# In the first attention of a perceiver kernel, the steps whose low halves VectorE makes move by one place

## The reference

```python
x = x + _L0_xattn_ref(_layernorm(x, axis=-1), ctx_1024, mask_SxS2_ik0, L0_xattn_W_q, L0_xattn_W_k, L0_xattn_W_v, L0_xattn_W_o)
...
x = x + _L1_xattn_ref(_layernorm(x, axis=-1), ctx_1024, L1_xattn_Wq, L1_xattn_Wk, L1_xattn_Wv, L1_xattn_Wo, L1_xattn_bo)
```

## Time and profile before

| | |
|---|---|
| time, median of 3 runs | 423.71 us (423.68 to 423.8) |
| profiled execution, its own time | 421.03 us |
| its span | 419.0 us |
| PE busy | 385.3 us, 92% |
| DVE busy | 317.9 us, 76% |
| ACT busy | 287.4 us, 69% |
| POOL busy | 203.5 us, 49% |
| low halves on POOL (L589) | 67 of 1892 ns |
| low halves on DVE (L589) | 25, median 1083 ns, mean 1214 ns |

### The profile page before, as it was taken

One profiled execution on the slowest core, in us unless ns is written; L12 is line 12 of the kernel. 1 busy time (PEld: TensorE's weight loads), 2 busy tenths in 40 slices (PEclk: granted clock), 3 DMA queues, 4 the chain that ended last, 5 costly groups with the idle time before them and its releaser, 6 DMA issues.

```text
span 419.0 us, 11758 instructions
## 1 busy us (share of the span) xinstructions
PE 385.3 (92%) x4649; PEld 300.2 (72%) x4649; DVE 317.9 (76%) x868; ACT 287.4 (69%) x569; POOL 203.5 (49%) x128
## 2 busy tenths in 40 slices
PE   6788999999999999998988999999999998999975
PEld 3356777777767778887965677767777777888774
DVE  3788888888886887735769999999988887544544
ACT  3377888888787886645428798888899886533240
POOL 2467879879865551001001558889666660030000
PEclk9799999999999999999999999999999999999989
DMA  8889798999999998970004999999999999600000
GB/s 314 311 235 179 134 175 133 178 142 184 237 172 233 226 164 159 408 285 0 5 0 88 170 155 197 200 195 181 200 193 191 190 193 196 265 2 3 4 0 5
DMA packets 186567, 68.11 MB, mean 163 GB/s; under 512 B 181376, under 2 KB 182160, under 8 KB 185616
## 3 DMA queue, kind: packets, MB, share of 16 engines
q1 hardware_dynamic: 186224, 66.31, 78.5%
q10 hardware_dynamic: 288, 1.05, 0.7%
HBM read 21.90 MB, written 0.03 MB: 52 GB/s over the span
## 4 chain that ended last, share of the span: by engine, by line
PE 43%; DVE 29%; issue 9%; ACT 8%; DMA 7%; POOL 2%; SPq 1%; DVEq 0%; POOLq 0%; ACTq 0%
PE ps L519 14%; DVE probs L613 14%; PE ps L487 12%; DMA probsT<-halves 5%; ACT probs L556 3%; PE ps L748 3%; DVE probsT L642 3%; DMA moe<-in_ctxT 2%; DVE U L631 2%; PE ps L499 2%; PE ps L1080 2%; DVE den L626 2%; ACT halves L563 1%; DVE halves L589 1%; PE ps L1186 1%
## 5 line engine op out<-in xcount | busy, mean ns | idle before, releaser
L589 POOL TENSOR_TENSOR halves<-probs,halves 128x896 f16<-128x896 f32 x67 | 126.6, 1892 | 81.5 <-ACT halves L563 80.7
L519 PE MATMUL ps<-ctxN,probsT 128*128 128x128 f16 x2352 | 149.1, 219 | 4.7 <-DMA probsT<-halves 3.3
L487 PE MATMUL ps<-ctxT_parts,GT_parts 128*128 128x512 f16 (+1 forms) x660 | 143.5, 354 | 10.7 <-DVE negmax L613 10.2
L519 PEld LDWEIGHTS ps<-ctxN,probsT 128*128 128x128 f16 x2352 | 139.7, 98 | 17.7 <-DVE U L631 4.7
L556 ACT ACTIVATE probs<-probs,shifted 128x896 f32<-128x896 f32 x112 | 115.5, 1031 | 12.3 <-DVE shifted L618 12.2
L487 PEld LDWEIGHTS ps<-ctxT_parts,GT_parts 128*128 128x128 f16 x660 | 59.2, 98 | 62.6 <-DVE negmax L613 14.9
L563 ACT CAST halves<-probs 128x896 f16<-128x896 f32 x92 | 84.9, 922 | 0.0
L613 DVE CUSTOM_DVE_ANT_0 probs<-ps,maskb,negmax 128x896 f32<-128x896 f32 x56 | 67.5, 1205 | 2.6 <-PE ps L480 1.3
L613 DVE CUSTOM_DVE_ANT_0 probs<-ps,zero,negmax 128x896 f32<-128x896 f32 x56 | 67.4, 1204 | 0.3 <-issue 0.2
L631 DVE SCALAR_TENSOR_TENSOR U<-U,alpha,ps 128x128 f32<-128x128 f32 x112 | 38.3, 342 | 31.5 <-PE ps L519 31.5
L553 ACT ACTIVATE alpha<-negmax 128x1 f32<-128x1 f32 x96 | 28.2, 294 | 42.0 <-DVE negmax L613 41.1
(11 more groups left out here) (356 smaller groups left out, 362.7 us busy)
## 6 DMA issues: line engine op xcount, KB each, us to landing
moe<-in_ctxT SPq DMA_DIRECT2D x7, 448.0 KB, 7.6
moe<-in_mask SPq DMA_DIRECT2D x6, 448.0 KB, 10.3
moe<-in_gateT SPq DMA_DIRECT2D x2, 1024.0 KB, 9.8
moe<-in_upT SPq DMA_DIRECT2D x2, 1024.0 KB, 10.9
moe<-in_downT SPq DMA_DIRECT2D x2, 1024.0 KB, 12.9
moe<-in_fir_long SPq DMA_DIRECT2D x1, 2048.0 KB, 9.8
probsT<-halves SPq DMA_TRANSPOSE x92, 4.6
wv<-in_wv SPq DMA_DIRECT2D x2, 512.0 KB, 5.1
```

The lines of the kernel that those rows point to most:

```text
L487: ins = pe.matmul(ps[:, 2 * b + h, 0:width], GT_parts[:, g_part, r * P:(r + 1) * P], ctxT_parts[:, keys:keys + width], start=(g_part == 0 ...
L519: ins = pe.matmul(ps[:, bank, 0:D], probsT_parts[:, b, p_part, k * P:(k + 1) * P], ctxN_parts[:, at:at + D], start=(p_part == 0 and c_part ...
L589: eng.tensor_tensor(halves_of(L, n)[:, 1, :], probs[:, n % BUFS, :], halves_of(L, n)[:, 0, :], ALU.subtract).then_inc(lower_of(L, n)[0], 1)
```

## The change

Of the steps 4 to 29 of the first attention, VectorE makes the low halves of 6, 10, 14, 18, 22 and 26 in place of 5, 9, 13, 17, 21, 25 and 29. GpSimd makes the others: it loses six and gains seven. Steps 0, 2 and 52 stay on VectorE, and the second attention is as it was.

```diff
         def on_vector(L, n):
 
             if L == 0:
-                return n in (0, 2) or 4 <= n < 30 and n % 4 == 1 or n == STEPS - 4
+                return n in (0, 2) or 4 <= n < 30 and n % 4 == 2 or n == STEPS - 4
             return n % 4 == 3 or n in (0, 1, STEPS - 4)
```

## The result

The changed kernel takes 427.39 us in the median of 4 runs (424.8 to 428.27), the kernel before 423.75 (423.68 to 424.04). The ratio is 1.0095 (95% interval 1.007 to 1.012). A later set of runs gave 427.15 against 422.46, ratio 1.012 (1.0091 to 1.015). The change costs about 4 us.

The account below looks back on a forecast made before the run. The prediction took a 10.40 us loop through VectorE and TensorE as the bound. Meetings with GpSimd put max(29) 4.68 us later, idle time took back 0.7, and 4.0 on the median gave 427.7 us, range 425.5 to 429.5.

Parts of the forecast that it names:

- The bound of before: First attention, groups of four steps: a loop through VectorE and TensorE of 10.40 us, above TensorE's own 10.1.
- The new loop of 10.30: VectorE and ScalarE after the change: turned high half, cast and low half of 4k+2 make a group 10.30 us.
- M: Start of max(4k+1) on VectorE, from which a group's times are counted; lower(4k+2) may start at M + 8.87.
- The price of a meeting: VectorE's low half stands still until 0.13 us before GpSimd's ends, losing up to 1.64 us.
- All six: Meetings of VectorE's low halves of 6 to 26 with GpSimd's; groups with mask 11.94, upper 11.28, lower 10.37 us.
- The first rival: Meetings cost nothing or little, two L589 run side by side: 423.4 us, not slower; chance 0.10.
- The sum: max(29) 4.68 us later, less 0.7 of GpSimd idle time: lower(32) and the kernel 4.0 us later.
- The idle 0.99 of GpSimd: GpSimd's idle time before lower(32) in the kernel before takes 0.7 of the 4.68 us delay away.
- The end takes part back: Rival: TensorE's 1.41 us wait at step 34 absorbs delay, pv(34) only 2.6 later: 426.3 us; chance 0.13.
- Late transposes: Rival: transposes of 9 and 21, with 0.5 us of slack, delay TensorE: 430.5 us, or 429.1 for half; chance 0.12.

Follow-up runs that it names:

- experiment 2: Kernel before, with VectorE's low half one loop turn later, behind max(4k+4): 420.61 us against 422.64, ratio 0.9951.
- experiment 5: Kernel before, with all of GpSimd's context and mask jobs of chunks 2 to 6 done ahead of step 4: 457.79 us in one execution.
- experiment 7: Against the kernel before: VectorE one loop turn later, its steps 5, 9, 14, 17, 21, 26, 29 and 33: 421.23 us against 422.46, ratio 0.9965.
- experiment 6: Changed kernel, with all of GpSimd's context and mask jobs of chunks 2 to 6 done ahead of step 4: 455.21 us in one execution.
- experiment 1: Changed kernel, with VectorE's low halves of 6 to 26 one loop turn later: 421.27 us against 422.64 of the kernel before, ratio 0.9978.
- experiment 3: Kernel before, with only two of the moved steps, 9 to 10 and 21 to 22: 425.29 us against 422.64, ratio 1.0049.
- Experiment 11: Kernel before, with only the load of wo moved behind the transpose of step 34: 421.34 us against 422.46, ratio 0.9972.
- experiment 8: experiment 7 with the load of wo moved behind the transpose of step 34: 420.29 us against 422.46 of the kernel before, ratio 0.994.
- experiment 9: Changed kernel timed again without an edit: 427.15 us against 422.46 of the kernel before, ratio 1.012.
- Experiment 4: Changed kernel, VectorE's moved low halves made as a multiplication of probs by 1, one SBUF input: 424.36 us in one execution, against 422.64 before.

## Why the prediction was right

*The bound of before.* Right. A loop of 10.40 over VectorE and TensorE, and not TensorE alone: experiment 2 cut it and the groups without a ctxT_upper went at 9.94 to 10.00, experiment 5 showed 10.40 with GpSimd's jobs out of the way. TensorE's own pace is a little shorter than the 10.1 that I gave, the five groups of experiment 7 average 9.96.

*The new loop of 10.30.* Right within 0.01 us (experiment 6). Of its pieces, the low half could start at M + 8.85 (52.52 less 43.67) for the 8.87 that I gave.

*The price of a meeting.* It was the step that I held least sure, since the longest loss in the rows was 0.43. The rule of those rows, free 0.13 before the end of the other's L589, held up to 1.65: 54.30 - 0.13 = 54.17, and 54.17 + 1.08 = 55.25. All six were forecast within 0.2, the six L589 at 2.08, 2.73, 1.23, 2.08, 2.73, 1.23 against about 1.9, 2.7, 1.15, 2.1, 2.7, 1.15. Experiment 6, which moves GpSimd's jobs, takes the meetings away from step 10 on; experiment 1, which moves VectorE's part, leaves at most 0.27 us of each. The cost goes with them in both. What decides the sum is when GpSimd's low half ends, not who begins first: in experiment 3 VectorE began 0.57 behind GpSimd and not 0.11, and the group took 11.94 all the same. The first rival, that two L589 go side by side, is refuted.

*The sum.* From max(9) to max(29) 55.90 was forecast and 56.06 came. To compare places I count from max(5), before which the kernels are equal: max(5) stands at 32.93 before and at 32.39 after, so the span after began with 0.54 less. From there, lower(32) came 4.17 later (80.96 against 76.79) where I had said 4.0, and pv(34) 4.40 later (97.92 against 93.52), as the wait for the transpose grew from 1.41 to 1.66. Behind that nothing changed. The spans differ by 3.9, which is 4.4 less those 0.54. The medians differ by 3.6 in the first set of runs and by 4.7 in the second, so 4.0 is right within what they scatter, and that 427.4 came so near to 427.7 is in part luck.

*The idle 0.99 of GpSimd* before lower(32) took its part back, as said: the chain is unbroken from 103.20 to the mask at 115.33.

*The end takes part back.* No. TensorE's wait at pv(34) did not shrink. Experiment 11 shows what had made that transpose late and long: the load of wo ahead of it in SP's queue. In the changed kernel the load (122.12) and the transpose (123.69) both came later along with GpSimd.

*Late transposes.* No wait for them at pv(9) or pv(21) in the changed kernel. But the slack is as thin as I feared: the faster versions ran into waits of 0.7 to 0.9 us, and in experiment 8 one of them decided a race. A second trace of the changed kernel (experiment 9) has one of 1.17 at 117.41 that the first does not have. Its cause is open.

*What was missing* is in experiment 2's finding: the change takes VectorE's low half to a better place in its list and at the same time to a step whose high half is only just ready and whose neighbour is on GpSimd. I had the gain of the place, 0.3 us a group, and let the new loop take it away; that it can be had by itself I did not say. Taken apart, the place gains 2.0 us (experiment 2), some 0.4 a group, and the step, at that place, costs between 6 and 7 (420.61 against 427.15 and 427.39).

## What to carry to other kernels

When two engines share work on the same memory, draw both timelines over each other before moving an item: the price of a move is in who else is running then. Compute when each half becomes ready, when each engine is free, and who starts first. Here 0.1 us decided that VectorE and not GpSimd stood still for 1.6; by the prediction's reckoning the group would have been as long the other way, which no run tested. And separate the two things that a change of order does, which item and which place: here the steps of before, one loop turn later, gave 2.0 us (experiment 2), and even the steps of the change, put so, were no slower than the kernel before (experiment 1).

## What the runs showed of the hardware

A subtraction of two SBUF operands on VectorE (128x896, 1.08 us alone) that starts inside GpSimd's L589, L1359, L1360 or L1364 stands still until 0.13 or 0.14 us before that one ends (up to 1.65 here), and the next GpSimd instruction then waits for VectorE (L1359 2.53 for 1.68). With the cast L1360, which has one input, experiment 2 shows it: it ran from 71.32 to 72.25, and lower(17), begun at 71.50, lost 0.61. With L1364 experiment 3 does: 60.24 to 62.13, and lower(13), begun at 61.58, lost 0.42. The profile books the time of standing still as busy time of the instruction that is held, and not as a wait: the row of 2.73 has an idle time of 0.27 only, and on the page the mean of 1392 ns is the sign of it. The Trainium skill, page "SBUF — State Buffer", section "SBUF: two separate sides", says that the first comer holds the shared port pair for the whole instruction; the runs agree, but for the last 0.13, for L589, L1359, L1360 and L1364.

They do not agree for the mask job, a GpSimd instruction from int32 to bfloat16 with one input. Of its 3.22 us it holds VectorE up in the beginning alone. The first mask of the changed kernel in GpSimd's timeline, and the low half of step 2 in VectorE's (both below): begun 0.30 behind the mask, it lost 0.50. The kernel before has the same pair, a mask at 31.13 and a low half of 1.58 at 31.42, a meeting that the prediction left out. But there lower(9) at 50.20 lay in the middle of a mask from 48.44 and lost nothing.

```profile
30.59 3.22 POOL L1353 TENSOR_SCALAR maskb<-moe 128x896 bf16<-128x896 int32 x1
```

```profile
30.89 1.58 DVE L589 TENSOR_TENSOR halves<-probs,halves 128x896 f16<-128x896 f32 x1 [0.66 <-ACT halves L563]
```

The same page and section of the Trainium skill count VectorE instructions in a two-port mode among those that take the pair. Experiment 4 fits this, though no row names the mode: the multiplication by 1 ran at an estimated 0.6 us, nearly twice the pace, and lost as much as the subtraction.
